# One product for keys and values, and numerators and scores placed ahead of it

## The reference

```
x = x + linear_attention(layernorm(x))       # elu(q)+1, elu(k)+1; kv = kp^T v; num = qp kv; num / z; then o_w
x = x + softmax(scores(ctx, ctx) * layernorm(x), masked)   # scores from a projected context of 64 features
x = x + ffn(layernorm(x))                    # Hadamard, gate and up (1024), silu, Hadamard, down
```

## Time and profile before

| | us |
|---|---|
| median of 3 runs | 137.56 (137.55 to 137.78) |
| the profiled execution | 137.59 |
| its span, first to last instruction | 135.8 |
| TensorE busy in the span | 126.4 (93%) |
| VectorE, ScalarE, GpSimd busy | 80.2, 78.2, 71.3 |

### The profile page before, as it was taken

How to read it: one execution, slowest core, us unless ns; L and a number is a source line. 1 busy time by engine, 2 the same in 40 slices (tenths; PEclk the granted TensorE clock), 3 DMA queues, 4 the chain that set the end, 5 groups by cost and what they waited for, 6 DMA issues and landing times.

```text
span 135.8 us, 2669 instructions
## 1 busy us (share of the span) xinstructions
PE 126.4 (93%) x998; PEld 119.2 (88%) x998; DVE 80.2 (59%) x202; ACT 78.2 (58%) x165; POOL 71.3 (53%) x90
## 2 busy tenths in 40 slices
PE   6959999699999999799999999999999999999980
PEld 2438998699899999699999989999989999999980
DVE  0269489779957676955796876762726412423212
ACT  0467899487576559867663684457197630356300
POOL 4113799968999969664551344362145350054600
PEclk9999999999999999999999999999999999999997
DMA  3999985000000000000000110000200000200002
GB/s 57 328 254 389 390 250 190 0 0 2 2 5 0 0 5 2 0 0 0 5 0 0 39 39 5 0 2 5 77 0 2 0 0 5 77 0 5 0 0 77
DMA packets 4721, 7.52 MB, mean 55 GB/s; under 512 B 608, under 2 KB 2720, under 8 KB 4580
## 3 DMA queue, kind: packets, MB, share of 16 engines
q1 hardware_dynamic: 4190, 7.09, 15.8%
q10 hardware_dynamic: 518, 0.25, 0.9%
HBM read 6.29 MB, written 1.05 MB: 54 GB/s over the span
## 4 chain that ended last, share of the span: by engine, by line
PE 76%; DVE 8%; ACT 6%; DMA 4%; issue 3%; POOL 2%; POOLq 0%
PE bank L1104 31%; PE bank L1117 17%; PE bank L1008 7%; PE bank L981 4%; PE bank L1068 4%; DMA kvs<-in_bias 4%; PE bank L1090 3%; PE bank L1030 2%; PE bank L971 2%; PE bank L1040 1%; PE bank L1050 1%; PE bank L1076 1%; ACT xn L422 1%; PE bank L1012 1%; DVE sc_up L789 1%
## 5 line engine op out<-in xcount | busy, mean ns | idle before, releaser
L1104 PE MATMUL bank<-xh_home,wug 128*128 128x256 f32 x384 | 49.4, 284 | 0.0
L1104 PEld LDWEIGHTS bank<-xh_home,wug 128*128 128x128 f32 x384 | 47.3, 191 | 0.2
L305 POOL TENSOR_TENSOR hs<-front,hs 128x256 fp32r<-128x256 f32 x32 | 23.7, 747 | 32.8 <-ACT hs L526 32.8
L517 ACT ACTIVATE front<-bank,vecs 128x256 f32<-128x256 f32 x32 | 15.0, 472 | 19.1 <-PE bank L1104 19.1
L809 DVE SCALAR_TENSOR_TENSOR front<-bank,sc_up,front 128x256 f32<-128x256 f32 x32 | 15.2, 480 | 16.0 <-ACT front L517 16.0
L1117 PE MATMUL bank<-wdh,hs 128*128 128x256 f32 x192 | 23.8, 284 | 0.0
L1117 PEld LDWEIGHTS bank<-wdh,hs 128*128 128x128 f32 x192 | 23.4, 191 | 0.1
L526 ACT CAST hs<-front 128x256 fp32r<-128x256 f32 x32 | 12.8, 400 | 4.5 <-DVE front L809 4.4
L1008 PE MATMUL bank<-wqkv,xT 128*128 128x256 f32 x96 | 14.5, 289 | 0.0
L1008 PEld LDWEIGHTS bank<-wqkv,xT 128*128 128x128 f32 x96 | 12.7, 189 | 0.9 <-ACT xT L429 0.5
L646 DVE BATCH_NORM_STATS2 st<-x_res 128x6 f32<-128x256 f32 x24 | 9.0, 415 | 5.3 <-DMA x_res<-in_x 5.1
(11 more groups left out here) (103 smaller groups left out, 204.9 us busy)
## 6 DMA issues: line engine op xcount, KB each, us to landing
wd_a<-in_w_d SPq DMA_DIRECT2D x1, 1024.0 KB, 9.6
front<-in_w_ug SPq DMA_DIRECT2D x2, 512.0 KB, 10.8
back<-in_w_ug SPq DMA_DIRECT2D x2, 512.0 KB, 5.3
out<-x_res SPq DMA_DIRECT2D x8, 128.0 KB, 1.9
wd_b<-in_w_qkv SPq DMA_DIRECT2D x3, 256.0 KB, 5.1
x_res<-in_x SPq DMA_DIRECT2D x1, 512.0 KB, 8.1
back<-in_ctx_t SPq DMA_DIRECT2D x1, 260.0 KB
x_res<-in_x SPq DMA_DIRECT2D x1, 256.0 KB, 6.7
```

The source lines that it names most:

```text
L305: g.tensor_tensor(hs[:, 1, n % JB, :], sg[:, n % RING, :], hs[:, 0, n % JB, :].bitcast(F32), ALU.subtract)\
L517: a.activation(sg[:, n % RING, :], B("GU", n)[:, 0:SEQ], ACT.Silu, scale=vecs[:, V_WSUG + JB + j:V_WSUG + JB + j + 1]).then_inc(s["sg"], 1)
L1104: ins = mm(dst[:, n * SEQ:(n + 1) * SEQ], wug[:, wa, k, at_col + j * P:at_col + (j + 1) * P], xh[b][:, xb, k, :], start=(i == 0), stop=(i ...
```

## The change

Keys and values become one step KV: a product has 512 columns (keys 0 to 255, values 256 to 511), and each half of the tokens has its own bank. For that the weights lie side by side. ScalarE reads each bank twice (256 columns of exp, 256 of copy), VectorE once per bank. KV stands in `HEAD` where K stood, save that NUM(0) and SC(0) go ahead of KV(1), and SC(2) and NUM(1) ahead of KV(2). At the start the bias of keys and values is split in one go, and the value weights are split ahead of the tokens of batch 0. ScalarE's list has `keys_values(b)` where `exp_k(b)` stood, save that `score_evac(2)` and `prob(0)` go ahead of `keys_values(2)`. VectorE does `attend(1)` ahead of `logits(0)`.

```
-HEAD = (("T1", 0), ("K", 0), ("mx", 0), ("V", 0), ("Q", 0), ("u", 0), ("T1", 1), ("ST", 0), ("u", 1), ("K", 1),
-        ("SC", 0), ("NUM", 0), ("V", 1), ("AT", 0), ("T1", 2), ("Q", 1), ("OUT", 0), ("ST", 1), ("K", 2), ("NUM", 1),
-        ("V", 2), ("SC", 2), ("AT", 1), ("Q", 2), ("T1", 3), ("OUT", 1), ("SC", 3), ("T3", 0), ("K", 3), ("SC", 1),
-        ("XH", 0), ("V", 3), ("Q", 3), ("ST", 2))
+HEAD = (("T1", 0), ("KV", 0), ("mx", 0), ("Q", 0), ("u", 0), ("T1", 1), ("ST", 0), ("u", 1), ("NUM", 0), ("SC", 0),
+        ("KV", 1), ("AT", 0), ("T1", 2), ("Q", 1), ("OUT", 0), ("ST", 1), ("SC", 2), ("NUM", 1), ("KV", 2),
+        ("AT", 1), ("Q", 2), ("T1", 3), ("OUT", 1), ("SC", 3), ("T3", 0), ("KV", 3), ("SC", 1), ("XH", 0),
+        ("Q", 3), ("ST", 2))
...
-        wqkv = sb("wqkv", [P, 2, 3, FB, HID], F32R)
+        wqkv = sb("wqkv", [P, 2, FB, 3 * HID], F32R)
...
-                    wait_full(sp, "K", 0)
+                    wait_full(sp, "KV", 0)
...
+            def keys_values(b):
+                for i in range(ST):
+                    cols = slice(i * HID, (i + 1) * HID)
+                    wait_full(act, "KV", b, i)
+                    if b:
+                        wait_read(act, "KV", b - 1, i)
+                    elif i == 0:
+                        act.wait_ge(s["fills"], 2)
+                    if b >= 2 and i == 0:
+                        wait_full(act, "ST", b - 2)
+                    a.activation(ek[:, cols], B("KV", b, i)[:, 0:HID], ACT.Exp, bias=neg1[:, :])
+                    a.copy(vx[:, b % 2, i * FB:(i + 1) * FB, 0:P], B("KV", b, i)[:, HID:2 * HID].rearrange("p (n e) -> p n e", e=P))\
+                        .then_inc(s["kv"], 1)
...
-            bias_hi(K_COLS)
+            bias_hi(KV_COLS)
             one_rows()
             w_hi("wk", 0)
+            w_hi("wv", 1)
             xT_hi(0)
-            w_hi("wv", 1)
             w_hi("wq", 2)
-            bias_hi(VQ_COLS)
+            bias_hi(Q_COLS)
             ctx_hi(0)
-            exp_k(0)
+            keys_values(0)
             mx_hi()
-            v_copy(0)
...
-            exp_k(1)
+            keys_values(1)
             mask_bias()
             negate_mean(1, 3)
             ug_hi(0)
-            v_copy(1)
             at_hi(0)
...
-            exp_k(2)
+            score_evac(2)
             prob(0)
-            v_copy(2)
-            score_evac(2)
+            keys_values(2)
...
             def elu_k(b):
+                for i in range(ST):
+                    dve.wait_ge(s["kv"], ST * b + i + 1)
+                    if b >= 2 and i == 0:
+                        wait_full(dve, "ST", b - 2)
+                    v.scalar_tensor_tensor(kp[:, b % 2, i, :], ek[:, i * HID:(i + 1) * HID], 1.0, B("KV", b, i)[:, 0:HID],
+                                           ALU.min, ALU.max).then_inc(read_of("KV", b, i), 1)
...
-            bias_lo(0, K_COLS)
+            bias_lo(0, KV_COLS)
             normalise1(0)
             w_lo(0)
+            w_lo(1)
             xT_lo(0)
-            w_lo(1)
             w_lo(2)
-            bias_lo(1, VQ_COLS)
+            bias_lo(1, Q_COLS)
...
+            attend(1)
             logits(0)
-            attend(1)
...
+            def kv_proj(b):
                 pe.wait_ge(s["xT_hi"], b + 1)
                 if b == 0:
+                    pe.wait_ge(s["w_hi"], 2)
+                for i in range(ST):
+                    dst = take("KV", b, i)
                     for n, (k, wa, xb) in enumerate(X_PASSES):
                         if b == 0 and i == 0 and wa:
+                            pe.wait_ge(s["w_lo"], 2)
                         if i == 0 and xb:
                             wait_read(pe, "T1", b)
+                        mm(dst[:, :], xT[:, b % 2, xb, k, i * P:(i + 1) * P], wqkv[:, wa, k, 0:2 * HID], start=(n == 0), stop=False)
                     if b == 0 and i == 0:
+                        pe.wait_ge(s["bias"], 1)
                         pe.wait_ge(s["ones"], 1)
+                    done(mm(dst[:, :], ones[:, 0:P], bias_r[:, 0:2 * HID], start=False, stop=True), "KV", b, i)
```

More of the change, by code:

```diff
@@ L41 @@
 V_SUG, V_SUD, V_WSUG, V_COLS = 0, 2, 10, 26
-K_COLS, VQ_COLS = slice(0, HID), slice(HID, 3 * HID)
+KV_COLS, Q_COLS = slice(0, 2 * HID), slice(2 * HID, 3 * HID)
 UG_ORDER = (0, 2, 1, 3)
@@ L71, in banks_of @@
 def banks_of(group, i):
-    return [(group, i, t) for t in range(2)] if group in ("NUM", "Y") else [(group, i, 0)]
+    return [(group, i, t) for t in range(2)] if group in ("KV", "NUM", "Y") else [(group, i, 0)]
 def schedule():
@@ L206, in decoder_kernel @@
                  "ug_hi ug_lo fly pre_hi pre_lo wd_hi "
-                 "xT_hi ek eq z_eps z_inv at_hi "
+                 "xT_hi kv eq z_eps z_inv at_hi "
                  "sx logit prob rsum x2 y "
@@ L407, in w_hi @@
                 act.wait_ge(ld[name], 16)
-                a.copy(wqkv[:, 0, c], qkv_raw[:, c]).then_inc(s["w_hi"], 1)
+                a.copy(wqkv[:, 0, :, c * HID:(c + 1) * HID], qkv_raw[:, c]).then_inc(s["w_hi"], 1)
             def bias_hi(cols):
@@ L570, in _ @@
             x3_hi(0)
-            exp_k(3)
+            keys_values(3)
             ug_hi(2)
@@ L574, in _ @@
             prob(1)
-            v_copy(3)
             ug_hi(3)
@@ L684, in w_lo @@
                 dve.wait_ge(s["w_hi"], c + 1)
-                v.tensor_tensor(wqkv[:, 1, c], qkv_raw[:, c], wqkv[:, 0, c].bitcast(F32), ALU.subtract).then_inc(s["w_lo"], 1)
+                cols = slice(c * HID, (c + 1) * HID)
+                v.tensor_tensor(wqkv[:, 1, :, cols], qkv_raw[:, c], wqkv[:, 0, :, cols].bitcast(F32), ALU.subtract).then_inc(s["w_lo"], 1)
             def xT_lo(b):
@@ L993, in turn3 @@
                 turn("T3", b, xn3)
-            def kv_proj(name, b, c):
-                dst = take(name, b)
-                cols = slice(c * HID, (c + 1) * HID)
+            def kv_proj(b):
                 pe.wait_ge(s["xT_hi"], b + 1)
                 if b == 0:
-                    pe.wait_ge(s["w_hi"], c + 1)
+                    pe.wait_ge(s["w_hi"], 2)
                 for i in range(ST):
-                    into = dst[:, i * HID:(i + 1) * HID]
+                    dst = take("KV", b, i)
                     for n, (k, wa, xb) in enumerate(X_PASSES):
                         if b == 0 and i == 0 and wa:
-                            pe.wait_ge(s["w_lo"], c + 1)
+                            pe.wait_ge(s["w_lo"], 2)
                         if i == 0 and xb:
                             wait_read(pe, "T1", b)
-                        mm(into, xT[:, b % 2, xb, k, i * P:(i + 1) * P], wqkv[:, wa, c, k, :], start=(n == 0), stop=False)
+                        mm(dst[:, :], xT[:, b % 2, xb, k, i * P:(i + 1) * P], wqkv[:, wa, k, 0:2 * HID], start=(n == 0), stop=False)
                     if b == 0 and i == 0:
-                        pe.wait_ge(s["bias"], c + 1)
+                        pe.wait_ge(s["bias"], 1)
                         pe.wait_ge(s["ones"], 1)
[L1012 to L1019, removed]
+                    done(mm(dst[:, :], ones[:, 0:P], bias_r[:, 0:2 * HID], start=False, stop=True), "KV", b, i)
             def q_proj(b):
@@ L1029, in q_proj @@
                     for n, (k, wa, xb) in enumerate(PASSES):
-                        mm(into, wqkv[:, wa, 2, k, m * P:(m + 1) * P], xT[:, b % 2, xb, k, :], start=(n == 0), stop=False)
+                        mm(into, wqkv[:, wa, k, 2 * HID + m * P:2 * HID + (m + 1) * P], xT[:, b % 2, xb, k, :], start=(n == 0), stop=False)
                     ins = mm(into, bias_r[:, 2 * HID + m * P:2 * HID + (m + 1) * P], ones[:, :], start=False, stop=True)
@@ L1034, in state @@
             def state(b):
-                wait_read(pe, "K", b)
-                wait_read(pe, "V", b)
+                for i in range(ST):
+                    wait_read(pe, "KV", b, i)
                 dst = take("ST", b)
@@ L1130, in down @@
                     done(block_products(i, JB - 1), "Y", b, i)
-            steps = {"mx": weights_product, "u": project, "T1": turn1, "SC": scores, "K": k_proj, "V": v_proj, "Q": q_proj,
+            steps = {"mx": weights_product, "u": project, "T1": turn1, "SC": scores, "KV": kv_proj, "Q": q_proj,
                      "ST": state, "NUM": numerator, "AT": turn_at, "OUT": o_proj, "T3": turn3, "XH": hadamard_x, "WD": w_down}
```

## The result

The changed kernel is slower: median 142.19 us (141.70 to 142.71, 4 runs) beside 137.61 (137.55 to 137.78, 4 runs), ratio 1.033 (95% interval 1.028 to 1.038). Its executions come in two kinds a microsecond apart, 141.70 and 141.73, 142.66 and 142.71, and the median lies between them; the profiled one is of the longer, 142.71, span 140.9.

The account below looks back on a forecast made before the run. The prediction took TensorE from T3(1) on, with other engines' waits setting AT(0), to bound the kernel. Start -0.4, mask +2.15, behind AT(0) -0.1 gave 139.2 us; the clock's 1.2 made 140.4, range 138.6 to 141.3.

Parts of the forecast that it names:

- the mechanism: Late mask_bias delays attend(0) and AT(0), TensorE idles 3.5 us and its clock falls: 140.4 us, chance 0.58.
- The sum without the clock: Whole kernel at unchanged clock: start -0.4, mask +2.15, between AT(0) and T3(1) -0.1, together +1.65 us.
- The first failed step: KV(1)'s second bank full at 23.1, mask_bias from 23.85 to 25.75, so AT(0) at 26.65, 1.75 us late.
- The second failed step: From AT(0) through OUT(0): 2.95 us at half clock would lose 1.45 us; 1.2 taken, lower end 0.7.
- Products: 28 narrow products per batch become 14 wide ones at 0.2275 us: 0.17 us saved per batch, 0.67 in all.
- Start: KV(0) begins 0.45 us late at 10.2, but later steps run 0.4 earlier, u_lo(1) at 19.2 for 19.62.
- Behind AT(0): From AT(0) to T3(1): NUM(1) waits 0.4 us, T1(3) nothing, T3(1) 0.9; the stretch adds -0.1 us.
- slack takes the delay up: Rival: idle stretches before T1(3) and T3(1) absorb most of the late mask, +0.35, 137.9 us; chance 0.11.
- the reason given for softmax(1): SC(1), behind a whole KV(3), is full at 46.3 and sets softmax(1), which starts at 50.5.
- GpSimd's shift_of(1, 3): Behind mask_bias and negate_mean(1, 3), it slides by some 1.4 us, still in time for rstd_of(2, 0).
- Clock stays: Rival: mask late before AT(0) but TensorE's clock does not fall, 139.2 us, range 138.7 to 139.7; chance 0.23.
- The mask is in time: Rival: mask_bias ends before VectorE's reciprocals at 23.6, the start's 0.4 us gain stays, 137.2 us; chance 0.08.

Follow-up runs that it names:

- experiment 3: Changed kernel with 13 added 512-column products, overwritten later, keeping TensorE busy between KV(1) and AT(0): 140.20 us beside 137.50.
- experiment 1: Changed kernel with only mask_bias() moved ahead of keys_values(1) in ScalarE's list: 137.56 us beside 137.50.
- experiment 2: Kernel before, with only v_copy(1) moved up ahead of mask_bias(): four executions at 139.50, 140.97, 141.06 and 141.99 us, beside 137.50.
- experiment 8: Changed kernel with mask_bias() ahead of keys_values(1), normalise(3, 1) ahead of pre_hi(1), and SC(1) ahead of KV(3): 138.63 us beside 137.49.
- experiment 10: Changed kernel with mask_bias() ahead of keys_values(1), pre_hi(0) of negate_mean(3, 1), ug_hi(2) of keys_values(3), logits(1) of xh_lo(0): 136.70 us beside 137.43.
- experiment 5: Changed kernel with only TensorE's order undone, KV(1) and KV(2) back where K(1) and K(2) stood: 142.61 us beside 137.50.
- experiment 4: Changed kernel with 6 added products between KV(1) and AT(0): three executions at 140.22 to 140.34 us, three at 141.74 to 141.81, beside 137.49.

## Why the prediction was wrong

The direction, the mechanism and the place were right. Two terms of the sum were too small, and the time fell 0.9 us above the range's upper end. The sum without the clock gave +1.65 us, and experiment 3 shows +2.7 (140.20 beside 137.50). For the clock the sum took 1.2, and it cost 1.5 or 2.5. The executions that lost 1.5 would have stayed in the range with 139.2 (140.7), so both terms failed together.

*The first failed step: when KV(1) is full, and AT(0) with it.* The links are as forecast, and 0.6 later. The step is KV(1)'s second bank, "the second at 19.9 + 3.2 = 23.1"; it was full at 23.74. NUM(0) started at 18.60, not 18.25, because diagonal(0) ended at 18.50; NUM(0) and SC(0) took 1.87 us in the chain, not 1.65; KV(1) took 3.27, not 3.2. Then mask_bias ran from 24.4 for 23.85, and AT(0) started at 27.27 for 26.65, that is 2.37 us late for 1.75. Of the 1.0 us that the sum without the clock lacks, 0.6 arise here and 0.3 behind AT(0) (below). Experiments 1 and 2 show the mask from both sides: with only the mask put back in time all of the loss is gone, and a late mask alone costs the kernel before 2.0 us.

*The second failed step: the clock's cost.* That it falls was right, and so were the 3.54 us of idle (3.5). The step is "That much at half pace loses 1.45 us [...] I take 1.2". It took the 2.95 us of the first warm-up for the whole length, read from the pace of the weight loads; the granted clock reads 1.00 there, so the two are not the same measure. Here the clock stayed at 0.50 for 6.8 us, 5.6 of them with work, and cost 2.54. In the shorter kind it cost about 1.5. Experiment 3 shows both costs (142.7 and 141.7 against 140.2), experiment 2 likewise (141.0 and 142.0 against 139.5).

*Products.* The trace has 1.40 us for six wide products, 0.233 each, where the sum took 0.2275 from another 512-column step, WD (L1076 in the earlier trace rows). 14 take 3.26 us, 0.1 less than before per batch and 0.4 in all, not 0.67.

*Start.* KV(0) began at 10.03 (10.2 forecast), u_lo(1) at 19.40, which is 0.22 earlier, not 0.4.

*Behind AT(0).* NUM(1) waited 0.53 (0.4), T1(3) nothing, T3(1) 1.06 (0.9), and the slide from AT(0) to T3(1), clock aside, was +0.23 (5.14 - 2.37 - 2.54) for -0.1. That slack takes the delay up was refuted. But the reason given for softmax(1) was wrong: not SC(1) but ScalarE's second read of KV(3), with ug_hi(2) and xh_hi(0) behind it, sets it (experiments 8 and 10). Its start in the kernel before was also misread by a tenth, 48.85 for the 48.95 of the earlier trace rows. GpSimd's shift_of(1, 3) slid by 2.0 us (26.55 for 24.57), not by 1.4, and was still in time.

*The rivals.* "Clock stays" would be 140.2 (139.2 forecast); none of the four runs showed it, but one of four did in experiment 2, at 139.50. "The mask is in time" was made true in experiment 1 and gave 137.56, not 137.2, because T3(1)'s wait covers the rest.

Why the half clock lasts 3.4 us in one execution and 6.8 in another stays open. The same program has both costs, so the program alone doesn't decide it. In the four traces that show a fall, the moment of the fall goes with the length: where the half clock lasted 6.8 us, it had fallen while TensorE idled (26.0 and 25.7, ahead of AT(0) at 27.27 and 26.58), and where it lasted 3.4, it fell after TensorE had taken up work again (28.6 behind 27.33, 41.4 behind 40.81). But the first two also had the longer idle stretches (3.54 and 3.39 us, against 2.17 and 2.48), so these four don't tell which of the two matters, and no experiment tests it. The shorter executions of the changed kernel and of experiment 2 have no trace.

## What to carry to other kernels

When two steps are joined, look in each in-order list at what stood between the two old ones and just behind: here a 1.9 us conversion that belonged to another chain now waited for the values as well. An idle stretch of TensorE can cost more than itself, since the products behind it may run at half the clock (seven of eight executions with 3.4 to 3.5 us of idle); count both, and give the second its own range. And ask of every saving which wait ends last ahead of it: the change, with its mask in time, was worth nothing until ScalarE's list ahead of T3(1) was shortened, and then some 0.25 us at most (136.70 against 136.94, with intervals of the two ratios that just overlap).

## What the runs showed of the hardware

By the executions' times and mean clocks, TensorE's clock fell behind idle stretches of 3.54 us in all four runs of the changed kernel, of 3.4 us in three of four, of 2.2 us in three of six, and of 2.48 us in experiment 5 (142.47 to 142.69, four runs). It did not fall behind 0.6 us in experiment 3 (four runs), nor behind the 1.90 us ahead of AT(0) in experiment 5's trace.

In the two traces where it fell during the idle stretch, that was 2.3 and 2.5 us after the last product had ended (23.73 and 23.19), and it stayed at 0.50 for 6.8 us, though TensorE worked without a break for the last 5.6 and 5.9 of them. In the traces of experiments 4 and 5 it fell 1.3 and 0.6 us after TensorE had taken up work again, and stayed at 0.50 for 3.4 us, all of it with work. The executions of the first kind lost 2.5 us to it; those of experiment 4 lost 1.5.
